# The order of two small GpSimd steps in a software-pipelined attention stage: scales of the branches and scale of the second norm

## The chip, the cores and the metric

The kernel runs on one core of one Trainium2 chip. The metric is the device time of one execution in microseconds (us), the median of several runs. TensorE is called PE, its weight loads PEld, VectorE DVE, ScalarE ACT, GpSimd POOL, SyncE SP, as in the profile.

## What is computed

The input x is 2 x 2048 x 128 in float32, so 4096 tokens of width 128. The layer is a linear attention block and a mixture of eight experts, each with a modulated norm in front and a gate behind:

```python
h = _layernorm(x) * (1 + ca) + sa
# attention block
q = h @ Wq;  feat = elu(q) + 1
msg = (feat @ KV) * Z            # KV and Z from sums over all tokens of a batch
msg = msg @ Wm
y   = h + _layernorm(msg, g1, b1)
mlp = relu(msg @ W1) @ W2
y   = y + _layernorm(mlp, g2, b2)
x   = x + ga * y
# expert block
h = _layernorm(x) * (1 + cb) + sb
x = x + gb * experts(h)          # 8 experts, one per token, chosen from softmax(h @ Wg)
```

The two layernorms inside the attention block (of `msg` and of `mlp`) are the two branches. The kernel needs, for each token, one scale 1/sqrt(mean square + eps) per branch, and then, from the finished x, the mean and the scale of the second norm.

## The kernel before, in words

The 4096 tokens are 32 tiles of 128 (one token per partition), in G = 8 groups of GT = 4 tiles. A first loop over the groups does the first norm, q and the features, and sums what KV needs. The **second loop**, which the change touches, is written out per engine as a software pipeline: each engine has a Python loop over rounds s, and in round s each step of that engine works on a group that is some rounds behind. The engines meet only at semaphores, and each engine runs its own list strictly in the order written. Behind the loop come the router (logits, softmax, a search of ten steps on DVE and ACT for the experts' thresholds), the placing of tokens in slots, and the expert stage with 28 gathers, 35 weight pieces and 28 scatters. None of these is edited.

The steps of the second loop, by group g:

- `qprime(g)` (POOL, L344 to L351) scales the features by z and gives `qp`; PE transposes it (`p_tq`), ACT copies it (`a_qT`, L492).
- PE: `p_y1(g)` (L749) makes branch 1 in bank pQ0, and behind it the hidden layer (L755); `p_y2(g)` (L766) makes branch 2. `p_y1(g)` waits for `u1_done` of group g-1.
- ACT: `a_square(g, 0)` and `a_square(g, 1)` (L501 to L508, four squares each, whose accumulators fill `ssq`) signal `sq1` and `sq2`; `a_relu(g)` (L498, L499) lies between them. `a_xn3(g)` (L523, four tiles) applies the second norm, and waits for `nm_done`.
- POOL: `yrs(g)` (L353 to L358) makes the branches' scales `yr` from `ssq` once `sq1` and `sq2` of group g are there: a small operation at L274 (`yv`) and a power at L275 (`yr`), 128 x 8. `rs3(g)` (L360 to L362) makes the second norm's scale `rs` from the variance in `mv` once `stats3` of group g is there: L274 (`ve`) and L275 (`rs`), 128 x 4.
- DVE: `v_xn3(g)` (L1115) waits for `rs3` and makes `nm`, minus mean times scale; `v_x1(g)` (L1117 to L1127) waits for `yr_done`, adds the two scaled branches to x (L1122, two passes of four tiles), and then takes the statistics of x (`bn` L977, `mv` L980, signal `stats3`); `v_u1`, `v_u2` (L1105, L1110) scale the branches by the rows of weights and free their PSUM banks.

The order in a round s is, per engine: ACT second norm of s-5, squares of branch 1 of s-2, relu of s-2, squares of branch 2 of s-3. DVE:

```python
if 0 <= s - 5 < G - 2:
    v_xn3(s - 5)
if 0 <= s - 4 < G - 1:
    v_x1(s - 4)
```

then `v_u1(s - 2)` and `v_u2(s - 3)`. So on DVE `nm` of a group stands in front of `x1` of the next group. On POOL a round is `qprime(s)`, `rs3(s - 4)`, `yrs(s - 3)`; in rounds 9 and 10 `yrs` stands in front of `rs3`.

Of the kernel before, what the change touches and what calls it, by code (L numbers as in the profile page):

```python
# [20 lines left out]
G = NT // GT  # L21
# [24 lines left out]
def build(nc, x, Wq, Wm, W1, W2, g1, b1, g2, b2, Wg, EW1, EW2, c, wmod, table, out):  # L46
    with ExitStack() as ctx:
# [8 lines left out]
        def sem(name):  # L56
            return ctx.enter_context(nc.semaphore(name))
# [125 lines left out]
        S = {n: sem(n) for n in names}  # L183
# [7 lines left out]
        def experts_of(engine, i):  # L191
            _, values = nc.values_load_multi_w_load_instructions(eid[0:1, i:min(i + RQ, NI)], engines=[engine])
            return [nc.s_assert_within(v, max(0, k - NP + 1), min(k, E - 1),
                                       skip_runtime_bounds_check_because="a piece's expert is counted from the experts' ends on the chip and"
                                                                         " lies between these for any input")
                    for k, v in enumerate(values, i)]
# [62 lines left out]
        def _(gp):  # L259
# [13 lines left out]
            def rsqrt(dst, src, tmp, scale, eps, width):  # L273
                link(gp.tensor_scalar(tmp, src, scale, eps, ALU.mult, ALU.add))  # L274
                return gp.tensor_tensor(dst, tmp, neghalf[:, 0:width], ALU.pow)  # L275
# [68 lines left out]
            def qprime(g):  # L344
                gp.wait_ge(S["z_done"], g + 1)
                if g >= 2:
                    gp.wait_ge(S["tq"], g - 1)
                gp.wait_ge(S["ft_done"], g + 1)
                gp.tensor_tensor(qp[:, g % 2, :].rearrange("p (t c) -> p t c", c=HD),  # L349
                                 bgroup(feat, g).rearrange("p t (h c) -> p (t h) c", c=HD),  # L350
                                 z[:, g % 2, :].unsqueeze(2).to_broadcast([P, GT * H, HD]), ALU.mult).then_inc(S["qp_done"], 1)  # L351

            def yrs(g):  # L353
                gp.wait_ge(S["sq1"], g + 1)
                gp.wait_ge(S["sq2"], g + 1)
                if g >= RY:
                    gp.wait_ge(S["x1_done"], g - RY + 1)
                rsqrt(yr[:, g % RY, :], ssq[:, g % RY, :], yv[:, g % RY, :], 1.0 / D, LN_EPS, 2 * GT).then_inc(S["yr_done"], 1)  # L358

            def rs3(g):  # L360
                gp.wait_ge(S["stats3"], g + 1)
                rsqrt(rs[:, g, :], mv[:, g, :, 1], ve[:, g, :], 1.0, LN_EPS, GT).then_inc(S["rs3"], 1)  # L362

            def rs3_half(h):
                g, ts = G - 1, slice(2 * h, 2 * h + 2)
                gp.wait_ge(S["stats3"], G + h)
                rsqrt(rs[:, g, ts], mv[:, g, ts, 1], ve[:, g, ts], 1.0, LN_EPS, 2).then_inc(S["rs3"], 1)
# [8 lines left out]
            for s in range(G + 6):  # L376
                if s < G:
                    qprime(s)
                if s == G + 2:
                    yrs(G - 1)  # L380
                if s == G + 1:
                    yrs(G - 2)
                if 0 <= s - 4 < G - 1:
                    rs3(s - 4)
                if s - 4 == G - 1:
                    rs3_half(0)
                    rs3_half(1)
                if 0 <= s - 3 < G - 2:
                    yrs(s - 3)
            gp.wait_ge(S["keys"], 1)  # L390
            for g in range(DG):
                h2tok(g)


            gp.wait_ge(S["slots_done"], 1)
            gp.wait_ge(S["tab_done"], 16 * 2 * G)

            def gather(t):
                gp.indirect_dma_start(row[:, t, :], None, table[:, :], bass.IndirectOffsetOnAxis(gidx[:, t:t + 1], 0)).then_inc(gathered[t], 16)  # L399
# [1049 lines left out]
```

## Time and profile before

| | us |
|---|---|
| median of 3 runs | 280.78 |
| lowest, highest | 280.15, 281.31 |
| the profiled execution, its own time | 277.45 |
| span of the profiled execution (first to last instruction) | 275.7 |

The page gives the busy shares PE 68%, DVE 65%, ACT 45%, POOL 47% of the span. The second loop with `yr` and `rs` runs from about 60 to 119 us; the search follows from 129 us, the gathers from 172 us, and the expert pieces to the end. A timeline row reads: start, duration, engine, line, operation, destination<-sources, shapes, count, and in brackets the idle time of the engine in front and who ended it. Several equal instructions in a row are one row (x4); its duration reaches from the first one's start to the last one's end. An ACT square with an accumulator shows as two rows, the second a read of the accumulator.

### The profile page before, as it was taken

The page shows a single profiled execution, that of the slowest core. Times are in us where ns is not written, and L with a number is a line of the kernel's source. Part 1 is how long each engine was busy: PE and PEld are TensorE (multiplying, and loading weights), DVE is VectorE, ACT ScalarE, POOL GpSimd, SP SyncE. Part 2 cuts the span into 40 slices and gives each one's busy share as a digit, 9 for nine tenths or more (in the row PEclk, how much of TensorE's full clock was granted, in tenths as well). Part 3 has the DMA queues.
Part 4 walks back from the last instruction along what each step waited for, and adds up shares of the span by engine and source line. Part 5 has one row for each costly group of instructions (what it writes and reads, how often), then busy time and mean ns, then how long its engine had stood idle before and what let it go on. Part 6 is the DMA issues. An engine that isn't in the chain of part 4 may idle for free.

```text
span 275.7 us, 4416 instructions
## 1 busy us (share of the span) xinstructions
PE 188.1 (68%) x1151; PEld 147.9 (54%) x1151; DVE 177.9 (65%) x660; ACT 124.2 (45%) x392; POOL 129.9 (47%) x207
## 2 busy tenths in 40 slices
PE   0788989796997797676758697751004995966740
PEld 0546759575776577671526275541004984856640
DVE  2779979999977666948898889900001895433340
ACT  2159964465597777435777642311001342232210
POOL 8737303142555445511995000777771037545572
PEclk9999999999799799555575999997555899899895
DMA  5892000001000000000567100434331334443310
GB/s 156 217 322 69 2 1 2 0 0 39 2 0 1 2 0 1 0 2 0 152 179 210 32 4 0 136 116 132 99 110 51 102 88 139 130 117 115 117 39 29
DMA packets 22009, 20.09 MB, mean 73 GB/s; under 512 B 2464, under 2 KB 19360, under 8 KB 21984
## 3 DMA queue, kind: packets, MB, share of 16 engines
q1 hardware_dynamic: 18752, 14.03, 17.2%
q0 software_dynamic: 2240, 5.51, 6.6%
q10 hardware_dynamic: 992, 0.27, 0.8%
q8 instruction: 10, 0.16, 0.3%
q14 instruction: 15, 0.12, 0.1%
HBM read 13.51 MB, written 6.29 MB: 72 GB/s over the span
## 4 chain that ended last, share of the span: by engine, by line
DVE 36%; PE 31%; another core or an unknown queue 11%; POOL 9%; issue 7%; ACT 4%; POOLq 1%; DVEq 0%
PE pQ L938 7%; PE pH L929 6%; DVE scr L1241 6%; DVE x_sb L1122 5%; DVE bn L977 2%; DVE t L1074 2%; POOL out_dram L402 2%; POOL yr L275 2%; PE pQ L648 2%; PE pH L755 2%; POOL rs L275 2%; DVE x_sb L1075 2%; DVE rows L985 2%; PE pQ L842 1%
## 5 line engine op out<-in xcount | busy, mean ns | idle before, releaser
L402 POOL DMA_INDIRECT out_dram<-rows,gidx x28 | 28.4, 1015 | 34.6 <-DVE rows L1389 28.2
L938 PE MATMUL pQ<-ew,u 128*128 (+1 forms) x140 | 25.6, 311 | 27.7 <-DVE dig L1413 21.0
L399 POOL DMA_INDIRECT rows<-table_dram,gidx x28 | 27.7, 988 | 31.5 <-DVE gidx L1333 23.3
L614 ACT ACTIVATE u<-pH 128x256 f32<-128x256 f32 x35 | 13.5, 386 | 58.5 <-remote 27.4
L938 PEld LDWEIGHTS pQ<-ew,u 128*128 128x128 f32 x140 | 21.4, 218 | 30.2 <-issue 28.3
L929 PE MATMUL pH<-x_sb,hid 128*128 (+1 forms) x140 | 25.7, 313 | 9.1 <-issue 7.9
L1381 DVE SCALAR_TENSOR_TENSOR t<-pQ,wslot,scr 128x128 f32<-128x128 f32 x35 | 12.3, 351 | 26.7 <-PE pQ L938 19.4
L929 PEld LDWEIGHTS pH<-x_sb,hid 128*128 128x128 f32 x140 | 21.5, 220 | 10.8 <-issue 10.7
L349 POOL TENSOR_TENSOR scr<-feat,z 128x512 f32<-128x512 f32 x8 | 9.6, 1202 | 23.0 <-DVE z L1101 23.0
L1365 DVE COPY inv<-pL 128x105 f32<-128x105 f32 x1 | 0.3, 269 | 30.4 <-remote 30.4
L755 PE MATMUL pH<-qT,mall 128*128 128x512 f32 x32 | 17.8, 686 | 0.0
L506 ACT ACTIVATE sqj<-pQ 128x128 bf16<-128x128 f32 x60 | 15.7, 275 | 4.7 <-PE pQ L749 2.4
L274 POOL TENSOR_SCALAR ve<-mv 128x4 f32<-128x4 f32 (+1 forms) x17 | 3.6, 209 | 30.1 <-DVE mv L980 27.7
L275 POOL TENSOR_TENSOR rs<-ve,neghalf 128x4 f32<-128x4 f32 (+1 forms) x17 | 16.6, 977 | 1.4
L523 ACT ACTIVATE rows<-x_sb,nm,rs 128x128 f32<-128x128 f32 x30 | 12.5, 486 | 10.7 <-DVE nm L1115 10.2
L977 DVE BATCH_NORM_STATS2 bn<-x_sb 128x6 f32<-128x128 f32 x60 | 13.1, 281 | 5.3 <-DMA x_sb<-in_L_attn_x_dram 5.1
L766 PEld LDWEIGHTS pQ<-w,hid 128*128 128x128 f32 x112 | 13.8, 193 | 4.0 <-issue 4.0
L1122 DVE SCALAR_TENSOR_TENSOR x_sb<-scr,yr,x_sb 128x128 f32<-128x128 f32 x28 | 11.1, 456 | 7.0 <-POOL yr L275 7.0
L373 POOL TENSOR_TENSOR t<-rows,cbR 128x512 f32<-128x512 f32 x7 | 8.9, 1267 | 11.4 <-DVE khi L1231 10.5
L749 PE MATMUL pQ<-mall,qT 128*128 128x128 f32 x64 | 9.5, 295 | 6.6 <-DVE scr L1105 6.6
L275 POOL TENSOR_TENSOR yr<-yv,neghalf 128x8 f32<-128x8 f32 x8 | 13.5, 1692 | 0.7
L766 PE MATMUL pQ<-w,hid 128*128 128x128 f32 x112 | 13.6, 275 | 0.0
(316 smaller groups left out, 526.9 us busy)
## 6 DMA issues: line engine op xcount, KB each, us to landing
hid<-in_L_ffn_W_dram SPq DMA_DIRECT2D x35, 128.0 KB
table_dram<-x_sb SPq DMA_DIRECT2D x9, 256.0 KB, 2.8
x_sb<-in_L_attn_x_dram SPq DMA_DIRECT2D x8, 256.0 KB, 7.5
table_dram<-rows SPq DMA_DIRECT2D x7, 256.0 KB, 2.3
ew<-in_L_ffn_W_dram SPq DMA_DIRECT2D x2, 512.0 KB, 8.5
w1d<-in_L_ffn_W_dram SPq DMA_DIRECT2D x1, 1024.0 KB, 9.8
rows<-table_dram,gidx POOLq DMA_INDIRECT x28
out_dram<-rows,gidx POOLq DMA_INDIRECT x28
```

What stands on the lines that cost most here:

```text
L275: return gp.tensor_tensor(dst, tmp, neghalf[:, 0:width], ALU.pow)
L399: gp.indirect_dma_start(row[:, t, :], None, table[:, :], bass.IndirectOffsetOnAxis(gidx[:, t:t + 1], 0)).then_inc(gathered[t], 16)
L402: gp.indirect_dma_start(out.rearrange("b l d -> (b l) d"), bass.IndirectOffsetOnAxis(gidx[:, t:t + 1], 0), row[:, t, D:2 * D], None).then_ ...
L506: last = act.activation(sqj[:, g % 2, k * GT + t, :], (y2_bank(g) if k else pQ0)[:, t * D:(t + 1) * D], ACT.Square, accum_out=ssq[:, g % R ...
L614: act.activation(eh[:, i % 2, :], pH[i % 2][:, 0:F], ACT.Gelu).then_inc(S["eh_done"], 1)
L755: mm = te.matmul(pH[f][:, :], mall[:, b, D + f * P:D + (f + 1) * P], qT[:, g % 2, :], start=True, stop=True)
L766: mm = te.matmul(y2_bank(g)[:, t * D:(t + 1) * D], hid[:, g % 2, f, t * P:(t + 1) * P], w2[:, f, :], start=(f == 0), stop=(f == 1))
L929: mm = te.matmul(pH[i % 2][:, f * P:(f + 1) * P], wcur[:, i % RW, f * P:(f + 1) * P], xt[:, bass.ds(i - e, 1), :], start=True, stop=True)
L938: mm = te.matmul(pQ[i % 2][:, 0:D], eh[:, i % 2, f * P:(f + 1) * P], ew[:, bass.ds(e, 1), f * D:(f + 1) * D], start=(f == 0), stop=(f == 1))
L977: last = dve.bn_stats(bn[:, g, t, :], x_sb[:, g * GT + t, :])
L1122: last = dve.scalar_tensor_tensor(x1, u[:, t, :], yr[:, g % RY, n + t:n + t + 1], x1, ALU.mult, ALU.add)
L1241: last = dve.tensor_scalar(junk[:, j, :], keys, cur[:, k, j:j + 1], None, ALU.is_lt, ALU.add, accum_out=cnt[:, j:j + 1])
```

## The change

In every round the branches' scales of group s-3 are made in front of the second norm's scale of group s-4. Rounds 9 and 10 had that order, and round 3 has no `rs3`; so the order changes in rounds 4 to 8. Beside it, two waits in front of the first gather change places with each other.

```diff
             for s in range(G + 6):
                 if s < G:
                     qprime(s)
-                if s == G + 2:
-                    yrs(G - 1)
-                if s == G + 1:
-                    yrs(G - 2)
+                if 0 <= s - 3 < G:
+                    yrs(s - 3)
                 if 0 <= s - 4 < G - 1:
                     rs3(s - 4)
                 if s - 4 == G - 1:
                     rs3_half(0)
                     rs3_half(1)
-                if 0 <= s - 3 < G - 2:
-                    yrs(s - 3)
             gp.wait_ge(S["keys"], 1)
             for g in range(DG):
                 h2tok(g)
 
 
+            gp.wait_ge(S["tab_done"], 16 * 2 * G)
             gp.wait_ge(S["slots_done"], 1)
-            gp.wait_ge(S["tab_done"], 16 * 2 * G)
```

POOL's list, rounds 5 and 6 in front of `qprime` of round 6 (L349 writes `qp`, which lies in `scr`; `pool` is the wait of the power for the operation in front of it). Before:

```order
L349 TENSOR_TENSOR scr<-feat,z 128x512 [waits ft_done,tq,z_done]
L274 TENSOR_SCALAR ve<-mv 128x4 [waits stats3]
L275 TENSOR_TENSOR rs<-ve,neghalf 128x4 [waits pool]
L274 TENSOR_SCALAR yv<-ssq 128x8 [waits sq2,sq1]
L275 TENSOR_TENSOR yr<-yv,neghalf 128x8 [waits pool]
```

The same place now:

```order
L349 TENSOR_TENSOR scr<-feat,z 128x512 [waits ft_done,tq,z_done]
L274 TENSOR_SCALAR yv<-ssq 128x8 [waits sq2,sq1]
L275 TENSOR_TENSOR yr<-yv,neghalf 128x8 [waits pool]
L274 TENSOR_SCALAR ve<-mv 128x4 [waits stats3]
L275 TENSOR_TENSOR rs<-ve,neghalf 128x4 [waits pool]
```

In each of the rounds 4 to 7 the pair of `yr` has moved in front of the pair of `rs`. POOL's list from `rs` of round 8 to `rs` of round 10 (there is no `qprime` any more), before:

```order
L274 TENSOR_SCALAR ve<-mv 128x4 [waits stats3]
L275 TENSOR_TENSOR rs<-ve,neghalf 128x4 [waits pool]
L274 TENSOR_SCALAR yv<-ssq 128x8 [waits x1_done,sq2,sq1]
L275 TENSOR_TENSOR yr<-yv,neghalf 128x8 [waits pool]
L274 TENSOR_SCALAR yv<-ssq 128x8 [waits x1_done,sq2,sq1]
L275 TENSOR_TENSOR yr<-yv,neghalf 128x8 [waits pool]
L274 TENSOR_SCALAR ve<-mv 128x4 [waits stats3]
L275 TENSOR_TENSOR rs<-ve,neghalf 128x4 [waits pool]
```

and now:

```order
L274 TENSOR_SCALAR yv<-ssq 128x8 [waits x1_done,sq2,sq1]
L275 TENSOR_TENSOR yr<-yv,neghalf 128x8 [waits pool]
L274 TENSOR_SCALAR ve<-mv 128x4 [waits stats3]
L275 TENSOR_TENSOR rs<-ve,neghalf 128x4 [waits pool]
L274 TENSOR_SCALAR yv<-ssq 128x8 [waits x1_done,sq2,sq1]
L275 TENSOR_TENSOR yr<-yv,neghalf 128x8 [waits pool]
L274 TENSOR_SCALAR ve<-mv 128x4 [waits stats3]
L275 TENSOR_TENSOR rs<-ve,neghalf 128x4 [waits pool]
```

Here only round 8's two pairs have changed places; the pairs of round 9 stand as before. The lists of PE, ACT, DVE and SP are the same in both kernels.

## Rows read from the trace of the kernel before

**Rows 1.** The page's head and its chain that ended last, by engine.
```profile
span 275.7 us, 4416 instructions
...
DVE 36%; PE 31%; another core or an unknown queue 11%; POOL 9%; issue 7%; ACT 4%; POOLq 1%; DVEq 0%
```

**Rows 2.** The page's costliest groups: busy, mean ns | idle before, and its releaser.
```profile
L523 ACT ACTIVATE rows<-x_sb,nm,rs 128x128 f32<-128x128 f32 x30 | 12.5, 486 | 10.7 <-DVE nm L1115 10.2
...
L1122 DVE SCALAR_TENSOR_TENSOR x_sb<-scr,yr,x_sb 128x128 f32<-128x128 f32 x28 | 11.1, 456 | 7.0 <-POOL yr L275 7.0
```

**Rows 3.** Timeline of POOL, round 5: start, us, operation, [idle before <-releaser].
```profile
76.64 0.20 POOL L274 TENSOR_SCALAR ve<-mv 128x4 f32<-128x4 f32 x1 [3.52 <-DVE mv L980]
...
78.02 0.20 POOL L274 TENSOR_SCALAR yv<-ssq 128x8 f32<-128x8 f32 x1
78.30 1.64 POOL L275 TENSOR_TENSOR yr<-yv,neghalf 128x8 f32<-128x8 f32 x1
79.90 1.06 POOL L349 TENSOR_TENSOR scr<-feat,z 128x512 f32<-128x512 f32 x1
```

**Rows 4.** Timeline of DVE, 71 to 110 us.
```profile
71.86 0.10 DVE L1115 SCALAR_TENSOR_TENSOR nm<-mv,rs 128x4 f32<-128x4 f32 x1
...
76.17 0.38 DVE L980 BATCH_NORM_AGGREGATE mv<-bn 128x2 f32<-128x6 f32 x4
...
78.13 0.10 DVE L1115 SCALAR_TENSOR_TENSOR nm<-mv,rs 128x4 f32<-128x4 f32 x1
79.97 1.92 DVE L1122 SCALAR_TENSOR_TENSOR x_sb<-scr,yr,x_sb 128x128 f32<-128x128 f32 x4 [1.74 <-POOL yr L275]
...
84.01 0.38 DVE L980 BATCH_NORM_AGGREGATE mv<-bn 128x2 f32<-128x6 f32 x4
...
95.68 1.14 DVE L1122 SCALAR_TENSOR_TENSOR x_sb<-scr,yr,x_sb 128x128 f32<-128x128 f32 x4 [1.84 <-POOL yr L275]
...
101.12 0.16 DVE L1115 SCALAR_TENSOR_TENSOR nm<-mv,rs 128x4 f32<-128x4 f32 x1
...
109.63 0.16 DVE L1115 SCALAR_TENSOR_TENSOR nm<-mv,rs 128x4 f32<-128x4 f32 x1 [2.09 <-POOL rs L275]
```

**Rows 5.** Timeline of ACT, 72 to 106 us.
```profile
72.00 1.66 ACT L523 ACTIVATE rows<-x_sb,nm,rs 128x128 f32<-128x128 f32 x4 [4.77 <-DVE nm L1115]
...
76.43 0.25 ACT L506 ACTIVATION_READ_ACCUMULATOR sqj<-pQ 128x1 f32 x1
...
78.27 1.66 ACT L523 ACTIVATE rows<-x_sb,nm,rs 128x128 f32<-128x128 f32 x4
...
82.87 0.22 ACT L506 ACTIVATION_READ_ACCUMULATOR sqj<-pQ 128x1 f32 x1
...
101.31 1.65 ACT L523 ACTIVATE rows<-x_sb,nm,rs 128x128 f32<-128x128 f32 x4
...
105.94 0.22 ACT L506 ACTIVATION_READ_ACCUMULATOR sqj<-pQ 128x1 f32 x1
```

**Rows 6.** Timeline of POOL, round 9.
```profile
106.31 0.20 POOL L274 TENSOR_SCALAR yv<-ssq 128x8 f32<-128x8 f32 x1 [3.61 <-issue]
...
108.31 0.20 POOL L274 TENSOR_SCALAR ve<-mv 128x4 f32<-128x4 f32 x1
```

**Rows 7.** Timeline of PE, rounds 7 and 8.
```profile
85.11 1.13 PE L749 MATMUL pQ<-mall,qT 128*128 128x128 f32 x8 [1.48 <-DVE scr L1105]
86.08 1.88 PE L755 MATMUL pH<-qT,mall 128*128 128x512 f32 x4
...
92.99 1.60 PE L749 MATMUL pQ<-mall,qT 128*128 128x128 f32 x8 [1.52 <-DVE scr L1105]
94.37 3.14 PE L755 MATMUL pH<-qT,mall 128*128 128x512 f32 x4
```

**Rows 8.** Windows: length, busy (instructions) of PE, PEld, DVE, ACT, POOL, then PE clock.
```profile
94.00:96.00 2.00, 2.00 (x5) 1.05 (x5) 0.32 (x2) 2.00 (x9) 1.64 (x1) 0.50 0.03 8
```

**Rows 9.** Timeline of POOL, the first gather.
```profile
171.99 1.24 POOL L399 DMA_INDIRECT rows<-table_dram,gidx  x1 [23.27 <-DVE gidx L1333]
```

## The prediction

> **What bounds the kernel now.** I read the page's chain first: DVE carries most of it, and no engine is busy throughout [rows 1], so this is a kernel of waits and every stage is read by itself. Then the costliest groups: DVE's two passes that finish x waited 7.0 us for `yr`, and ACT's second norm waited some 10 us for `nm` [rows 2]. Both are in the second loop, and both waits end at POOL. The timelines of round 5 show how. POOL gets the statistics of group 1 and makes `rs(1)` from 76.64 on, then `yr(2)` from 78.02 to 79.94 [rows 3], and DVE starts `x1(2)` at 79.97 after 1.74 us of waiting [rows 4]. So the loop before is x1, statistics, rs, yr, x1. The reader is to see one more thing: `nm(1)` went out at 78.13, while POOL was still making `yr(2)` [rows 4], and ACT began its second norm at 78.27 [rows 5]. `rs` first gives ACT a start of almost 2 us on DVE.
>
> **What the change costs, step by step.** It adds and removes no operation. It moves five pairs: yr(1) to yr(5) now stand in front of rs(0) to rs(4). POOL waits in order, so `rs` is now held by all that `yr` waits for, that is by ACT's squares of both branches. DVE's list is unchanged and has `nm(g-1)` in front of `x1(g)`; so `x1(g)` still can't start before `rs(g-1)` is made. From one group to the next DVE needs both pairs either way. Their sum stays 3.32 us: from `yv` at 106.31 to `rs`'s first operation at 108.31 is 2.00 [rows 6], and from there to `nm` at 109.63 is 1.32 [rows 4, 6]. What changes is what the pairs wait for, and when ACT may go on.
>
> *Durations.* From `nm` to ACT's second norm 0.15 (78.13 to 78.27 [rows 4, 5]). From the second norm to the end of the squares of branch 2, with relu and the squares of branch 1 between, 4.68 (72.00 to 76.43 + 0.25 [rows 5]). Rounds 6 and 9 took 4.82 and 4.85 (78.27 to 83.09, 101.31 to 106.16 [rows 5]); I take 4.68, since in the other two ACT was early and had PE's branch 2 to wait for, and keep 4.85 as the upper bound. From the last square to `yv` 0.15 (106.16 to 106.31 [rows 5, 6]). Then 3.32.
>
> *Round 4.* yr(1) goes early, under DVE's own work. rs(0) may end some tenths later; `nm(0)` at 71.86 stands behind other DVE work by then. Cost 0.
>
> *Round 5.* ACT starts its second norm at 72.00 as before and ends the squares at 76.68, 0.13 behind the end of the statistics (76.17 + 0.38 = 76.55 [rows 4, 5]). So yr(2) starts at 76.83, and `nm(1)` goes out at 80.15 in place of 78.13: x1(2) is late by 0.3, but the second norm of ACT by 2.0.
>
> *Rounds 6 to 9.* Now a loop closes through ACT: `nm`, second norm, squares, yr, rs, `nm`. Its period is 0.15 + 4.68 + 0.15 + 3.32 = 8.30. In round 6 before, the squares of group 3 were done at 83.09, 1.3 ahead of the statistics at 84.39 [rows 4, 5]. That lead, which would have made the new order pay, was the gift of an early `nm`, and goes with it. DVE doesn't bind: from `nm` to the statistics is 4.5 (79.97 to 84.39, and 0.1), below the 4.83 of ACT. **One row shows the new period already:** in round 9 `yr` stands in front, and from `nm(4)` at 101.12 to `nm(5)` at 109.63 are 8.51 us, with 2.09 of DVE waiting for `rs` [rows 4].
>
> *Sum.* From `nm(0)` at 71.86 (unchanged) to `nm(5)` are five periods. Before: 109.63 - 71.86 = 37.77, or 7.55 each [rows 4]. After: 5 x 8.30 = 41.50, `nm(5)` at 113.36. **The loop ends 3.7 us later.** With 8.51 for each it would be 4.8. With POOL's answer to the squares as quick as to the statistics (76.55 to 76.64, 0.09 for my 0.15 [rows 3, 4]) it is 8.24 each and 3.4. I take 3.6, between the last and the first. Behind `nm(5)` the order is as before, and each stage waits for the one in front: POOL's first gather waited 23.27 us for the slots' addresses from DVE [rows 9], so the delay passes on whole. The two waits in front of that gather are both needed, and their order costs nothing; the later one decides.
>
> *A rule against the trace.* `qprime` ran beside the first pass of x1(2), which took 1.92 us; without it, in group 4, the pass took 1.14 [rows 3, 4]. The collision stays in the new order, as `qprime` and x1 are both released by the end of POOL's second pair, and costs the same 0.78 in both kernels. The Trainium skill (SBUF — State Buffer, Who interferes with whom) says that a VectorE operation with two SBUF inputs and a GpSimd operation that reads SBUF exclude each other, and the later one blocks for the whole instruction. With `nm` now between `rs` and x1, `qprime` (1.06 [rows 3]) would surely be first, and by the rule groups 2 and 3 would each lose up to 0.28 more: the sum would be 4.2 in place of 3.6. The trace shows 0.78 and I keep it.
>
> **Forecast.** The profiled execution took 277.45 and would take 281.05. The runs shown have a median 3.33 above it; a shift in one stage adds to either, so the time is 280.78 + 3.6 = **284.4 us**. A measurement of this kernel can tell some 0.5% (1.4 us) from no change.
>
> **Rivals.**
> - *The scales leave DVE's loop, faster.* The place is the wait of x1 for `yr`. If the squares of group g are done over 2.0 us ahead of the statistics of g-1, yr costs nothing, and the loop is x1, statistics, rs: 4.42 + 0.09 + 1.32 + 0.1 = 5.9, or DVE's own work of about 6.2 (from `nm(0)` to `nm(1)` 6.27 with hardly a wait [rows 4]). All the 7.0 us of waiting [rows 2] would go: 273.8. It decides at a lead of zero: above, x1 gains it, below it loses. For it: a lead of 1.3 in round 6. Against: round 5's lead is -0.13, and every later one comes from an earlier `nm`. Chance 0.05.
> - *No change.* The later second norm hides in ACT's waiting (some 10 us [rows 2]), or the delay is lost in the gathers. Then x1's 0.3 of round 5 is all: 281.1. Against: round 9 shows the period with ACT's waiting gone. Chance 0.08.
> - *Slower by more.* PE waits longer between groups and is granted its lower clock once or twice more. In round 8 it had stood for 1.52, and its clock was 0.50 of full speed (1.2 GHz) at 94 to 96 us [rows 7, 8]; the two steps took 1.60 and 3.14 in place of 1.13 and 1.88, 1.73 more [rows 7]. In round 7 it had stood for 1.48 and kept the clock. One more such stretch, mostly hidden as ACT is the later one, costs 0 to 1.7; with the long period of 8.51 that is 4.8 to 6.5: 285.6 to 287.3, and I put 286.0. Chance 0.14.
> - *The forecast*, 284.4 (its own range 283.6 to 285.6: 3.4 to 4.8, less 0.6 at the low end for the spread of the runs). Chance 0.73.
>
> **Range and chances.** The low end is the forecast's with the short period, 284.2, less 2.0, since the runs shown spread over 1.2 and the profiled one lies 3.3 below them; the high end is the middle of the third rival: 282.2 to 286.4. It leaves out the first two rivals and part of the third. Faster by over 0.5%: 0.05. Within: 0.08. Slower by over 0.5%: 0.87.
>
> **What would show it.** In the profile after: yr(2) starts at about 76.8 right behind ACT's squares; rs follows each yr without a gap; DVE's waits at L1122 for `yr` are gone, and in their place stand waits at L1115 for `rs` of about 2 us in rounds 6 to 9; x1 starts 0.1 behind `nm`; the periods of `nm` are 8.2 to 8.5; ACT's wait for `nm` is longer per round, with nothing of PE ending last at its squares; the stage from `nm(5)` to the end is as long as before. Wrong would be: squares done ahead of the statistics by 1 us or more in rounds 6 to 8, or a second loop as long as before.

## The result, and the profile after

| | before | after |
|---|---|---|
| median of 4 runs each, same chip (us) | 281.04 | 287.22 |
| lowest, highest | 280.15, 281.52 | 285.95, 287.81 |
| the profiled execution, its own time | 277.45 | 287.81 |
| its span | 275.7 | 286.1 |

The ratio is 1.0265 [1.0215, 1.0316], with its 95% interval in brackets: slower by 6.2 us, where 3.6 was forecast. In the experiments below, executions over 1.5% longer than the fastest of the same kernel are left out of medians and ratios, and of three kernels whose profiled execution was such a one (`qprime_gate`, `best`, `best_2`) only stages are read from it, not the whole time.

The spans differ by 10.4, but before was profiled in an execution 3.6 below its median and after in one 0.6 above its own; 10.4 - 3.6 - 0.6 is the same 6.2.

The page after; the first line is the chain that ended last, by engine, and answers to [rows 1]; the second is the group of ACT's second norm, which answers to [rows 2]:

```profile
DVE 20%; PE 15%; another core or an unknown queue 13%; issue 5%; ACT 3%; POOL 2%; DVEq 1%; DMA 1%; POOLq 0%; SPq 0%; ACTq 0%
...
L519 ACT ACTIVATE rows<-x_sb,nm,rs 128x128 f32<-128x128 f32 x30 | 12.4, 484 | 19.7 <-DVE nm L1111 19.4
```

The chain sums to some 60% here and to 100% before, so its shares can't be set against each other, and I read stage by stage. The second line can: ACT now waits 19.4 us for `nm` in place of 10.2. DVE's group of the x1 passes, which waited 7.0 us for `yr`, no longer stands among the page's costliest groups. The waiting went from DVE's x1 to ACT's second norm, as foretold.

The timeline of POOL after, rounds 5 and 6, against [rows 3]:

```profile
77.12 0.20 POOL L274 TENSOR_SCALAR yv<-ssq 128x8 f32<-128x8 f32 x1 [3.70 <-ACT sqj L502]
77.40 1.64 POOL L275 TENSOR_TENSOR yr<-yv,neghalf 128x8 f32<-128x8 f32 x1
79.12 0.20 POOL L274 TENSOR_SCALAR ve<-mv 128x4 f32<-128x4 f32 x1
79.41 1.01 POOL L275 TENSOR_TENSOR rs<-ve,neghalf 128x4 f32<-128x4 f32 x1
80.38 1.06 POOL L349 TENSOR_TENSOR scr<-feat,z 128x512 f32<-128x512 f32 x1
86.32 0.20 POOL L274 TENSOR_SCALAR yv<-ssq 128x8 f32<-128x8 f32 x1 [4.88 <-ACT sqj L502]
```

POOL waits for the squares of ACT, `rs` follows `yr` without a gap, and `qprime` (L349) follows `rs` without a gap. The timeline of DVE after, against [rows 4]; the passes of x1 in rounds 7 to 9, all 1.13, are left out:

```profile
72.15 0.10 DVE L1111 SCALAR_TENSOR_TENSOR nm<-mv,rs 128x4 f32<-128x4 f32 x1
...
80.45 1.01 DVE L1111 SCALAR_TENSOR_TENSOR nm<-mv,rs 128x4 f32<-128x4 f32 x1 [2.21 <-POOL rs L275]
81.38 1.13 DVE L1118 SCALAR_TENSOR_TENSOR x_sb<-scr,yr,x_sb 128x128 f32<-128x128 f32 x4
...
89.65 1.01 DVE L1111 SCALAR_TENSOR_TENSOR nm<-mv,rs 128x4 f32<-128x4 f32 x1 [2.28 <-POOL rs L275]
...
98.85 0.16 DVE L1111 SCALAR_TENSOR_TENSOR nm<-mv,rs 128x4 f32<-128x4 f32 x1 [2.75 <-POOL rs L275]
...
107.19 0.16 DVE L1111 SCALAR_TENSOR_TENSOR nm<-mv,rs 128x4 f32<-128x4 f32 x1 [2.75 <-POOL rs L275]
...
115.54 0.16 DVE L1111 SCALAR_TENSOR_TENSOR nm<-mv,rs 128x4 f32<-128x4 f32 x1 [2.75 <-POOL rs L275]
```

Here is the first thing that the prediction had wrong. The periods of `nm` are 8.30, 9.20, 9.20, 8.34 and 8.35. Three are the forecast's 8.30. The other two are 0.9 longer, and each begins with an `nm` that took **1.01** us where it takes 0.10 or 0.16 elsewhere. The two long ones are those with a `qprime` in front: it started at 80.38, `nm` at 80.45, and both end at 81.4. The x1 pass behind it then took 1.13, not the 1.92 of [rows 4]. `qprime` now hits the small operation that stands first, and ACT waits for that one. Timeline of ACT after, against [rows 5]:

```profile
81.50 1.65 ACT L519 ACTIVATE rows<-x_sb,nm,rs 128x128 f32<-128x128 f32 x4 [3.04 <-DVE nm L1111]
```

It starts 1.05 behind the start of `nm`; before, 78.13 to 78.27 was 0.14 [rows 4, 5]. The five periods sum to 43.39 against 37.77: **+5.6** in place of the forecast's +3.6 or +3.7.

The second thing stands at the gathers, against [rows 9]; timelines of DVE and of POOL after:

```profile
178.95 0.21 DVE L1329 TENSOR_REDUCE gidx<-pG 128x28 int32<-128x56 f32 x1
...
220.22 0.27 DVE L1361 COPY inv<-pL 128x105 f32<-128x105 f32 x1 [33.25 <-remote]
```

```profile
180.06 1.47 POOL L395 DMA_INDIRECT rows<-table_dram,gidx  x1 [25.44 <-DVE gidx L1329]
```

and of DVE before, the operation that makes the addresses and the later one at the slots' inverse table `inv`:

```profile
171.47 0.21 DVE L1333 TENSOR_REDUCE gidx<-pG 128x28 int32<-128x56 f32 x1
...
209.89 0.27 DVE L1365 COPY inv<-pL 128x105 f32<-128x105 f32 x1 [30.40 <-remote]
```

The first gather starts 1.11 behind the start of `gidx` after, and 0.52 before (171.47 to 171.99 [rows 9]), and takes 1.47 for 1.24. So the exchanged waits delay the first gather by 0.6, where I had put nothing. 5.6 + 0.6 = 6.2 is the difference of the medians, but that is a fit and not a measurement: the two profiled executions also differ by 1.6 from `nm(5)` to `gidx` (61.84 and 63.41) and by 3.0 from `gidx` to the first scatter (table below), and neither kernel was profiled again on this chip. The 5.6 of the loop is shown; how the rest of the 6.2 splits is not.

### The profile page after: what moved, and what is told of

Read it like the earlier page. It is cut to its first block, busy times and chain, and to the rows that moved or that the text cites. A ratio compares the mean times of both kernels' runs of the same rounds, so it can differ in the third digit from the quotient of the medians.

```text
span 286.1 us, 4416 instructions
## 1 busy us (share of the span) xinstructions
PE 198.0 (69%) x1151; PEld 153.4 (54%) x1151; DVE 178.4 (62%) x660; ACT 123.0 (43%) x392; POOL 129.0 (45%) x207
## 4 chain that ended last, share of the span: by engine, by line
DVE 20%; PE 15%; another core or an unknown queue 13%; issue 5%; ACT 3%; POOL 2%; DVEq 1%; DMA 1%; POOLq 0%; SPq 0%; ACTq 0%
DVE scr L1237 5%; PE pQ L934 4%; PE pH L925 4%; POOL out_dram L398 2%; DVE scr L1355 1%; PE pQ L838 1%; PE pG L762 1%; DVE u L1397 1%; PE pQ L828 1%; DVE x_sb L1130 1%; DVE x_sb L1118 1%; DVE featT L1321 1%; PE pF L828 1%; DVE cur L1251 1%
## 5 line engine op out<-in xcount | busy, mean ns | idle before, releaser
L925 PE MATMUL pH<-x_sb,hid 128*128 (+1 forms) x140 | 26.9, 323 | 22.6 <-issue 19.6
L925 PEld LDWEIGHTS pH<-x_sb,hid 128*128 128x128 f32 x140 | 22.2, 226 | 24.2 <-issue 23.9
L349 POOL TENSOR_TENSOR scr<-feat,z 128x512 f32<-128x512 f32 x8 | 9.7, 1209 | 25.0 <-DVE z L1097 25.0
L519 ACT ACTIVATE rows<-x_sb,nm,rs 128x128 f32<-128x128 f32 x30 | 12.4, 484 | 19.7 <-DVE nm L1111 19.4
L751 PE MATMUL pH<-qT,mall 128*128 128x512 f32 x32 | 18.4, 707 | 0.0
L274 POOL TENSOR_SCALAR yv<-ssq 128x8 f32<-128x8 f32 x8 | 1.6, 198 | 27.7 <-issue 15.6
L745 PEld LDWEIGHTS pQ<-mall,qT 128*128 128x128 f32 x64 | 8.6, 208 | 8.4 <-issue 7.3
## 6 DMA issues: line engine op xcount, KB each, us to landing
w1d<-in_L_ffn_W_dram SPq DMA_DIRECT2D x1, 1024.0 KB, 10.7
```

Source lines behind the costliest of these rows:

```text
L745: mm = te.matmul(pQ0[:, t * D:(t + 1) * D], qT[:, g % 2, t * P:(t + 1) * P], mall[:, b, 0:D], start=True, stop=True)
L751: mm = te.matmul(pH[f][:, :], mall[:, b, D + f * P:D + (f + 1) * P], qT[:, g % 2, :], start=True, stop=True)
L925: mm = te.matmul(pH[i % 2][:, f * P:(f + 1) * P], wcur[:, i % RW, f * P:(f + 1) * P], xt[:, bass.ds(i - e, 1), :], start=True, stop=True)
```

## The experiments

Four sets of kernels ran, on three chips (A, B twice, C), each set with the kernel before beside it. What follows: medians in us, the ratio to the kernel before on the same chip with its 95% interval.

| kernel | chip | before | this | ratio |
|---|---|---|---|---|
| after_again | A | 275.55 | 286.25 | 1.040 [1.036, 1.045] |
| waits_only | A | 275.55 | 280.38 | 1.019 [1.013, 1.024] |
| qprime_gate | A | 275.55 | 283.74 | 1.031 [1.025, 1.036] |
| turned_yr | A | 275.55 | 277.98 | 1.008 [1.005, 1.011] |
| before_again | B | 275.09 | 277.94 | 1.009 [1.003, 1.014] |
| loop_only | B | 275.09 | 282.32 | 1.024 [1.019, 1.029] |
| waits_memset | B | 275.09 | 281.41 | 1.019 [1.013, 1.025] |
| best | B | 275.09 | 270.51 | 0.983 [0.977, 0.990] |
| after_2 | B | 276.34 | 286.67 | 1.031 [1.024, 1.038] |
| waits_only_2 | B | 276.34 | 280.62 | 1.016 [1.010, 1.021] |
| loop_only_2 | B | 276.34 | 282.98 | 1.016 [1.009, 1.023] |
| best_2 | B | 276.34 | 271.02 | 0.975 [0.968, 0.983] |
| extra_tt | C | 279.78 | 287.58 | 1.023 [1.017, 1.029] |
| waits_three | C | 279.78 | 280.30 | 1.000 [0.995, 1.005] |
| old_waits_memset | C | 279.78 | 279.63 | 0.999 [0.994, 1.003] |
| best_rs_first | C | 279.78 | 279.61 | 0.998 [0.994, 1.002] |

The ratio is taken round by round, and so can differ from that of the medians, by 0.8% in `loop_only_2`. Differences in us below are of the medians, good to some 3 us across labels on chip B; where one carries weight, its ratio stands beside it.

### The two edits apart

`after_again` and `after_2` are the changed kernel. `waits_only` (and `waits_only_2`) is the kernel before with the two waits exchanged alone; `loop_only` (and `loop_only_2`) is the changed kernel with the waits in their old order:

```diff
+            gp.wait_ge(S["tab_done"], 16 * 2 * G)
             gp.wait_ge(S["slots_done"], 1)
-            gp.wait_ge(S["tab_done"], 16 * 2 * G)
```

> The changed kernel itself, beside the kernel before on the same chip. The profiled executions differ by 10.4 us of span, of which 5.6 lie between the first nm and nm(5) (43.39 against 37.77 us), none from nm(5) to the transposes of the probabilities (18.3 both), and 4.5 behind them. Theory A (only the second loop differs): 5.5 to 6.2 us slower, about 286.9 against 281.0; the stretch behind the search differs between executions of one kernel as much as between the kernels. Theory B (the stages behind are slower too): 8 us or more slower.

> The kernel before with only the two waits in front of the first gather in the new order. Theory A: no difference, within 0.3% of before (280.2 to 281.9), since both waits must be met and the slots' addresses come last. Theory B (some of the 6 us comes from there): 0.5 us or more slower.

> The changed kernel with the two waits in front of the first gather in the old order, so only the loop is changed. If the parts add: 5.6 us slower than before (five periods of 43.4 us against 37.8), and the stretch from the addresses to the copy is 38.4 us again. If the waits' order costs nothing and waits_only was chance: as slow as the changed kernel, 10 us on this chip.

> The kernel before, profiled again. If the two waits' order matters by itself (waits_only was 4.8 us slower than before in the median, and from the slots' addresses to the copy of the weights on DVE took 41.06 us there against 38.42), this execution shows again 38.4 us and 0.52 us from the addresses to the first gather. If it was chance, the stretch varies here too, up to 41 us.

On chip A the changed kernel was 10.7 us slower, more than the 6.2 on the first chip, and the exchanged waits alone were 4.8 slower. On chip B `loop_only` cost 7.2 (2.4%). So both edits cost, and the exchange can cost far more than the 0.6 read on the first chip. `before_again`, the same kernel text as the one beside it, came out 0.9% above it on chip B, 2.9 us by the medians: differences of that size across labels I don't read. In one set on chip B the sum was then tried:

> waits_only once more, now on one chip with the three below. Reading so far: with slots_done waited for behind tab_done the first gather starts 1.1 us behind the addresses in place of 0.5, on every chip; the rest of the stage was 4 us longer on two chips and equal on a third, where the kernel before takes 281 and not 276. So: if before takes about 276 here, 4 to 5 us slower; if about 281, 0 to 1 us slower.

> Only the loop changed: 5.6 to 6 us slower than before, whichever chip.

> The changed kernel: 5.6 us for the loop and what waits_only_2 shows: 10 us slower than before if that takes 276, 6.2 us if it takes 281; 286 to 288 in both cases.

+4.3 and +6.6 for the two edits, +10.3 for both; by the ratios 1.6% and 1.6%, and 3.1% for both. They add up, within the spread of a label, and the interval of each `loop_only` ratio holds the 5.6 of the loop. From the profiled executions, stages in us between rows (`nm(0)` to `nm(5)`; `gidx` to the first gather, to the copy `inv` on DVE, and to the first scatter; the last to the end):

| | chip | waits | nm to nm | to gather | to inv | to scatter | to end |
|---|---|---|---|---|---|---|---|
| before | first | old | 37.77 | 0.52 | 38.42 | 53.55 | 50.7 |
| after | first | new | 43.39 | 1.11 | 41.27 | 56.58 | 50.6 |
| before_again | B | old | 37.39 | 0.51 | 27.73 | 52.19 | 50.5 |
| loop_only | B | old | 43.40 | 0.51 | 24.89 | 51.92 | 49.3 |
| waits_only_2 | B | new | 37.72 | 1.11 | 41.01 | 56.25 | 50.4 |
| after_2 | B | new | 43.31 | 1.10 | 41.00 | 55.34 | 49.5 |
| old_waits_memset | C | old | 37.62 | 0.55 | 40.59 | 54.92 | 49.7 |
| waits_three | C | new | 37.81 | 1.10 | 41.25 | 56.51 | 50.8 |

The loop's length depends on the order of the pairs alone and the first gather on the order of the waits alone. Timelines of DVE and of POOL of `loop_only`, the changed loop with the old waits:

```profile
178.55 0.21 DVE L1329 TENSOR_REDUCE gidx<-pG 128x28 int32<-128x56 f32 x1
...
203.44 0.27 DVE L1361 COPY inv<-pL 128x105 f32<-128x105 f32 x1 [16.87 <-remote]
```

```profile
179.06 1.24 POOL L395 DMA_INDIRECT rows<-table_dram,gidx  x1 [24.77 <-DVE gidx L1329]
```

and of `waits_only`, the old loop with the new waits:

```profile
171.10 0.21 DVE L1333 TENSOR_REDUCE gidx<-pG 128x28 int32<-128x56 f32 x1
...
212.16 0.27 DVE L1365 COPY inv<-pL 128x105 f32<-128x105 f32 x1 [33.03 <-remote]
```

```profile
172.21 1.46 POOL L399 DMA_INDIRECT rows<-table_dram,gidx  x1 [23.81 <-DVE gidx L1333]
```

The copy `inv` waits 33 us for something that the trace does not name ("remote") with the new waits, and 16.9 with the old ones on chip B. With the new waits the time from `gidx` to it was 40.9 to 41.3 in all nine profiled executions, on every chip; with the old ones it was 23.4 to 27.7 in five on chip B, 38.4 on the first chip, 40.5 to 40.7 in three on chip C. `before_again` and `loop_only` had been expected to repeat the 38.4 and showed 27.7 and 24.9. So the exchange costs 4 to 5 us where the old order has the short form, and hardly anything where it has the long one anyway. It also fits the kernel before itself, 275 to 276 us on B, 280 on C and 281 on the first chip. That is a pattern over eighteen executions, not a cause; on chip A no kernel with the old waits was profiled.

Two more readings narrow it down. What the copy waits for in the code is the last `pL` matmul of PE. Timelines of PE, of before and then of `loop_only`:

```profile
183.83 0.86 PE L947 MATMUL pL<-featT 128*128 128x105 bf16 x14
```

```profile
190.72 0.86 PE L943 MATMUL pL<-featT 128*128 128x105 bf16 x14
```

By these rows PE was done at 184.7 and 191.6, 25 and 12 us ahead of the copy. So what comes late is not a long matmul but what lies between its row and the signal (the ends of matmuls are modelled). And in the long form the copy starts 2.0 to 4.7 us behind the end of the last gather's issue, in the short form 8.6 to 12.9 ahead of it.

### Does qprime block nm?

`qprime_gate` is the changed kernel, and `qprime` of groups 6 and 7 waits until `nm` has been made:

```diff
             def qprime(g):
+                if g >= 6:
+                    gp.wait_ge(S["nm_done"], g - 4)
```

> The changed kernel, with qprime of rounds 6 and 7 waiting for nm of the group that DVE makes in that round, so that it can't stand in front of nm. Theory A (nm was blocked for qprime's whole 1.06 us, in a loop that runs nm, second norm, squares, yr, rs, nm): nm(1) and nm(2) take 0.1 and not 1.01 us, their periods fall from 9.20 to 8.3, x1's first pass goes back to about 1.9 us but costs nothing, and the kernel is 1.85 us faster than the changed one: 4 us (1.4%) slower than before, 285.0. Theory C (PE's low clock sets the long periods): periods stay at 9.2 in the rounds with the low clock, and the time stays at that of the changed kernel.

Its timeline of DVE:

```profile
83.59 0.16 DVE L1113 SCALAR_TENSOR_TENSOR nm<-mv,rs 128x4 f32<-128x4 f32 x1 [2.18 <-POOL rs L275]
83.67 1.93 DVE L1120 SCALAR_TENSOR_TENSOR x_sb<-scr,yr,x_sb 128x128 f32<-128x128 f32 x4
...
91.94 0.16 DVE L1113 SCALAR_TENSOR_TENSOR nm<-mv,rs 128x4 f32<-128x4 f32 x1 [2.17 <-POOL rs L275]
```

`nm` is back at 0.16, the x1 pass at 1.93: the collision has moved off the loop. The periods are 8.28, 8.35, 8.33, 8.33, 8.33, in sum 41.62, against 41.50 in the prediction. It is 2.5 us faster than `after_again` on the same chip, 1.8 of which is the loop; the other 0.7 is within the spread. With qprime out of the way, the prediction's loop is measured nearly to the tenth.

`extra_tt` does the reverse. The changed loop with the old waits gets, in rounds 8 and 9, which have no `qprime`, one operation of its size whose result nobody uses (extra work, with the output unchanged):

```diff
                 if s < G:
                     qprime(s)
+                if s in (8, 9):
+                    gp.tensor_tensor(t2[:, :, :].rearrange("p t (h c) -> p (t h) c", c=HD),
+                                     bgroup(feat, G - 1).rearrange("p t (h c) -> p (t h) c", c=HD),
+                                     z[:, 1, :].unsqueeze(2).to_broadcast([P, GT * H, HD]), ALU.mult)
```

> The kernel with only the loop changed (loop_only), and in rounds 8 and 9, where there is no qprime, a tensor product of qprime's size and operands into a scratch tile, at qprime's place in POOL's order. It adds work that the reference doesn't have and leaves the output as it is. Theory A (a collision in front of nm costs its whole length in the ACT loop): nm(3) and nm(4) take 1.0 us in place of 0.16, their periods 9.2 in place of 8.35, the kernel 1.75 us slower than loop_only: 8 us slower than before, 284. If POOL's work at that place is free because POOL waits anyway: as loop_only, 282.3.

Its timeline of POOL, and then of DVE:

```profile
98.06 1.06 POOL L380 TENSOR_TENSOR t<-feat,z 128x512 f32<-128x512 f32 x1
```

```profile
98.13 1.01 DVE L1115 SCALAR_TENSOR_TENSOR nm<-mv,rs 128x4 f32<-128x4 f32 x1 [2.74 <-POOL rs L275]
107.30 1.01 DVE L1115 SCALAR_TENSOR_TENSOR nm<-mv,rs 128x4 f32<-128x4 f32 x1 [2.75 <-POOL rs L275]
116.47 0.16 DVE L1115 SCALAR_TENSOR_TENSOR nm<-mv,rs 128x4 f32<-128x4 f32 x1 [2.74 <-POOL rs L275]
```

The two `nm` that took 0.16 in rounds 8 and 9 now take 1.01, and the periods behind them are 9.17 each; the loop is 44.99, 1.6 longer than in `loop_only`. Against before on chip C it is 7.8 us slower by the medians, 6.4 by the ratio; its loop is 7.4 longer than the 37.62 of `old_waits_memset` on that chip. The cause of the missing 1.8 is settled from both sides.

The kernel before shows the same thing on x1. [rows 4] have its pass of four operations as one row of 1.92; a timeline of DVE before that ends at 81.0 us has the first of them alone:

```profile
79.97 1.13 DVE L1122 SCALAR_TENSOR_TENSOR x_sb<-scr,yr,x_sb 128x128 f32<-128x128 f32 x1 [1.74 <-POOL yr L275]
```

The other three took 0.34 each. So the whole collision fell on the one operation that stood first.

### Is it PE's clock?

The rival was a PE that waits longer and gets the lower clock. The hidden layer's four matmuls in rounds 7 and 8 (against [rows 7]), timeline of PE after:

```profile
86.69 1.88 PE L751 MATMUL pH<-qT,mall 128*128 128x512 f32 x4
...
96.77 3.62 PE L751 MATMUL pH<-qT,mall 128*128 128x512 f32 x4
```

and of `loop_only`, rounds 7 to 9:

```profile
86.39 3.39 PE L751 MATMUL pH<-qT,mall 128*128 128x512 f32 x4
...
95.59 1.88 PE L751 MATMUL pH<-qT,mall 128*128 128x512 f32 x4
...
104.16 3.35 PE L751 MATMUL pH<-qT,mall 128*128 128x512 f32 x4
```

Windows of after (the granted clock of PE is the third number from the right) show 1.00 in the first of its two and 0.50 in the second:

```profile
86.70:88.50 1.80, 1.80 (x7) 0.84 (x6) 0.64 (x3) 0.61 (x2) 1.72 (x2) 1.00 0.00 0
97.00:99.00 2.00, 2.00 (x3) 0.78 (x3) 0.15 (x2) 0.00 (x0) 1.65 (x3) 0.50 0.03 8
```

and in `loop_only` the clock was 0.50, 1.00, 0.50 (1.2, 2.4 and 1.2 GHz) at 87 to 89, 96 to 97 and 105 to 107 us. So the low clock fell in other rounds of the two, yet the periods of `nm` are equal: 8.30, 9.21, 9.19, 8.35, 8.35. Between 1.88 and 3.6 for these matmuls the loop doesn't change; ACT and POOL are later. The rival falls for the loop.

### What at the gathers costs 0.6?

Three kernels, all with the loop of before: `waits_memset` has the exchanged waits and a small operation of POOL behind them, `old_waits_memset` the old waits and the same operation, `waits_three` waits for the table, for the slots and for the table again.

```diff
+            gp.wait_ge(S["tab_done"], 16 * 2 * G)
             gp.wait_ge(S["slots_done"], 1)
-            gp.wait_ge(S["tab_done"], 16 * 2 * G)
+            gp.memset(jc[:, 0:1], 0.0)
```

```diff
+            gp.wait_ge(S["tab_done"], 16 * 2 * G)
             gp.wait_ge(S["slots_done"], 1)
             gp.wait_ge(S["tab_done"], 16 * 2 * G)
```

> The kernel before with the two waits in the new order and a memset of one column between them and the first gather. Theory D (a wait for the late signal that sits on the gather itself starts it late, as the engine prepares a gather only when its wait is met): the gather starts about 0.5 us behind the addresses and the time is that of before, 275.6 to 280.8. Theory E (the order of the waits doesn't matter, the long stretch is where instructions of DVE, ACT and PE are fetched behind the gathers' packets and that varies with any shift of the code): the time may be either, and the stretch may be 41 us with the gather starting as early as before.

> The kernel before, its two waits in the old order, and a memset of one column between them and the first gather. It delays the gathers by the memset alone. Theory F: no gain from the late signal's place is lost but the gather starts 0.7 us or more behind the addresses; if a start 0.5 us later alone makes the stage 4 us longer (another meeting of the gathers' packets with the fetches of instructions), the first scatter comes at 56 us; if the carried wait does it, at 52.5 to 54.

> The kernel before, which waits for tab_done, then slots_done, then tab_done again (the third wait is met by then). Five executions with the late signal (slots_done) waited for last began to gather 1.11 us behind the addresses and issued the first scatter 56.2 to 56.6 us behind them; four with tab_done last 0.5 us and 51.9 to 53.5. Theory F (the late signal must not be in the last wait, the one that the next instruction carries): as the old order, 0.5 us and 52 to 53.5 us. Theory G (the place of the late signal in the row of waits counts, not what follows): as the new order, 1.1 and 56.3 us.

From `gidx` to the first gather 1.14, 0.55 and 1.10 us. Timelines of DVE and of POOL of `waits_three`:

```profile
171.34 0.21 DVE L1334 TENSOR_REDUCE gidx<-pG 128x28 int32<-128x56 f32 x1
```

```profile
172.44 1.48 POOL L400 DMA_INDIRECT rows<-table_dram,gidx  x1 [23.84 <-DVE gidx L1334]
```

A memset between the waits and the gather changes next to nothing either way (1.14 and 0.55; I had expected 0.7 or more for the second), which speaks against a wait that is carried by the gather's own instruction. A repeated wait behind the late one doesn't bring back the 0.5 either. What all eighteen profiled executions have in common is one thing: 0.51 to 0.55 where the late signal, `slots_done`, is waited for first, and 1.10 to 1.14 where a wait that is already satisfied stands in front of it. Why stays open. On chip C `waits_three` came out 0.5 above before and `old_waits_memset` 0.2 below, both inside their intervals: there the 0.6 can't be told from nothing. On chip B `waits_memset` cost 1.9%, like `waits_only_2` with 1.6%.

Theory E above, that instructions fetched late set the long stretch, finds no support in the traces. They list the transfers of the `instruction` queues: the last of them in front of the copy `inv` ended 3.4 us ahead of it at the least (`after`), 18.8 in before, and 26.5 and 27.9 in `waits_only_2` and `best_rs_first`, which have the long form.

### An order of ACT and DVE in which the new order pays

If the loop goes through ACT's second norm, taking that off it should help. `turned_yr` is the changed kernel with ACT's second norm behind the squares of branch 1 and relu, and DVE's `v_u1` at the front of a round, so that PE is released earlier:

```diff
-                if 0 <= s - 5 < G - 1:
-                    a_xn3(s - 5)
...
                 if 0 <= s - 2 < G:
                     a_square(s - 2, 0, "y1_ready", "sq1")
                     a_relu(s - 2)
+                if 0 <= s - 5 < G - 1:
+                    a_xn3(s - 5)
...
             for s in range(G + 4):
+                if 0 <= s - 2 < G:
+                    v_u1(s - 2)
...
-                if 0 <= s - 2 < G:
-                    v_u1(s - 2)
```

> The changed kernel, with ACT's second norm moved behind squares of branch 1 and relu in its round, and DVE's scaling of branch 1 (u1) moved to the front of its round. Theory A: the squares no longer wait for nm, they are done ahead of the statistics, and the order of the change then pays: periods of nm of 6.3 to 6.6 us, second loop 4.3 us shorter than before, 276.7 us. Theory C: PE becomes the bound or falls to its low clock more often, and the time is between that of before and that of the changed kernel.

The periods fell to 6.3 to 7.2, in sum 33.40; two `nm` still took 1.05 and 1.06. But `nm(0)` came at 74.39 in place of 72.15, as `v_u1` in front delays the work of the early rounds, and the waits were the new ones: 277.98, still 2.4 above before, where 276.7 had been expected. `best` has the same moves with `v_u1` in front from round 5 on alone, the gate of `qprime`, and the old waits; `best_rs_first` has the moves of ACT and DVE on the kernel before, so `rs` first and no gate.

```diff
             for s in range(G + 4):
+                if s >= 5 and s - 2 < G:
+                    v_u1(s - 2)
...
-                if 0 <= s - 2 < G:
+                if 0 <= s - 2 < 3:
                     v_u1(s - 2)
```

> The order of the change in the loop, the old order of the two waits, ACT's second norm behind relu, DVE's scaling of branch 1 (u1) in front of its round from round 5 on, and qprime of rounds 6 and 7 behind nm. If squares no longer wait for nm, periods of nm are 6.3 us, nm(5) comes 6 us earlier than before, and the kernel is 6 us (2.1%) faster than before. If the old bound only gives way to PE or to its low clock: 3 us or less.

> ACT's second norm behind relu and DVE's u1 in front from round 5 on, as in the best version, but POOL in the old order (rs first; no gate on qprime). The old loop x1, statistics, rs, yr is still closed: periods of x1 of 7.8 us where qprime collides and 7.0 where not, nm(5) within 1 us of before, time 0 to 1 us below before. So the order of the change would be worth 5 us here, and cost 5.6 there. If the re-ordering of ACT and DVE is what gains, this is 4 us or more faster than before.

> The best version once more, in an execution that is not disturbed: 5 to 6 us faster than before, whichever chip, with nm(5) at 105.2 us from the span's start when nm(0) is at 72.

Timeline of DVE of `best_2`:

```profile
80.26 0.16 DVE L1113 SCALAR_TENSOR_TENSOR nm<-mv,rs 128x4 f32<-128x4 f32 x1
...
86.63 0.16 DVE L1113 SCALAR_TENSOR_TENSOR nm<-mv,rs 128x4 f32<-128x4 f32 x1
...
93.00 0.16 DVE L1113 SCALAR_TENSOR_TENSOR nm<-mv,rs 128x4 f32<-128x4 f32 x1 [0.60 <-POOL rs L275]
```

and of `best_rs_first`:

```profile
88.13 1.92 DVE L1122 SCALAR_TENSOR_TENSOR x_sb<-scr,yr,x_sb 128x128 f32<-128x128 f32 x4 [1.73 <-POOL yr L275]
...
95.95 1.14 DVE L1122 SCALAR_TENSOR_TENSOR x_sb<-scr,yr,x_sb 128x128 f32<-128x128 f32 x4 [1.84 <-POOL yr L275]
```

With `yr` first the first period is 7.75 and the other four are 6.33 to 6.37, in which DVE has little left to wait for; the sum is 33.15. With `rs` first DVE again waits 1.7 to 1.8 for `yr` in rounds 7 to 9, as in [rows 4], and the sum is 35.59. `best` is 4.6 and 5.3 us faster than before on chip B, in two sets (0.983 and 0.975), and beats both kernels; `best_rs_first` is level with before on chip C. So `yr` first costs 5.6 us of loop in one surrounding, and in the other, with the gate, it gains 2.4, where the expectation had 5. `turned_yr`, with `yr` first and no gate, has 33.40. Both kernels give some of it back later: from the search's start to `gidx` they take 44.9 to 45.0, `old_waits_memset` 42.3 and `before_again` 43.8. They ran on different chips, and `best` has the gate besides, so how its gain splits is not settled.

## Why the prediction was right and wrong

- **What bounds the kernel.** Right. DVE's waits at x1 went, and ACT's wait for `nm` grew from 10.2 to 19.4 us.
- **Round 5.** `yr(2)` was to start at 76.83 and `nm(1)` to go out 2.0 later, at 80.15. With `nm(0)` at 72.15 in place of 71.86 they came at 77.12 and 80.45: the same to the hundredth or two.
- **The period of 8.30.** Right for the mechanism as costed: 8.30, 8.34 and 8.35 in the rounds without a collision, and 41.62 for all five in `qprime_gate`, for 41.50. The row of round 9 before, 8.51, was the worse guide.
- **"A rule against the trace".** This step failed, and it is the larger miss: +1.8 of the loop. I saw that `nm` now stood between `rs` and x1, and that `qprime` would be first, but priced the collision on x1 alone: 0.78 kept, or 0.28 more per group by the rule. It fell on `nm`, which took 1.01 instead of 0.16, and `nm` is in the loop through ACT, which x1 is not. The cost of the old place doesn't count against it, because x1's share lies beside ACT's work once the loop goes through ACT: in `qprime_gate` the pass took 1.93 and the period stayed at 8.35. By 0.9 for each of two groups the sum would have been 3.7 + 1.8 = 5.5, for 5.6 measured. The Trainium skill (SBUF — State Buffer, Who interferes with whom) says that the later of the two is blocked for the whole instruction; the trace agrees, `nm` ends with `qprime`, at 81.46 and 81.44. It agrees before as well. `qprime` ended at 80.96 [rows 3], and the first x1 operation, alone in its row above, took 1.13 from 79.97 and ended just behind it, where one takes 0.34 otherwise. That is 0.79 more, and the 0.78 was the rule itself. I had read it as something milder.
- **"Their order costs nothing"** (the two waits). Failed: on the first chip the first gather started 0.6 later, and on two others the exchange cost up to 4.8 us. "The later one decides" was true of what is waited for and not of when the gather starts.
- **"The delay passes on whole".** Right within what can be read: from `nm(5)` to the search's start are 19.5 us in every kernel, so the loop's +5.6 arrives at the search whole. That +5.6 and +0.6 make up the +6.2 is a fit, as said with the result. From there to `gidx` the profiled executions vary by more than an edit explains: 42.32 and 43.77 for the same kernel, before and `before_again`.
- **The rivals.** The third had a range of 285.6 to 287.3 and would hold the time of 287.22, but by another mechanism: after has one low-clock stretch in these rounds as before had (96.77, and 94.37 in [rows 7]), and `loop_only`, with two, has the same periods. The first, a loop with the scales out of DVE's way, came near only once ACT's second norm was moved: 6.33 to 6.37 a period, where it said 5.9 to 6.2.

## What to carry to other kernels

Where an order changes, look at which operation now stands first behind a releaser that also releases a large one on another engine: a tiny operation in the critical loop can pay the large one's whole length, and the profile books that as its busy time, not as a wait. Before putting the scale that one engine waits for behind the one that another engine waits for, follow both loops through all engines: the order that loses here shortened the loop once ACT's second norm and DVE's `v_u1` had been moved. And exchange waits only on purpose, with the late signal waited for first as the default here.

## What was not expected of the hardware

- A DVE operation of 128 x 4 took 1.01 us beside a POOL operation of 1.06 with two inputs, and 0.10 or 0.16 without it: in all seven profiled executions of the new order without the gate it was so (1.01 to 1.06) wherever POOL's operation came just in front.
- Two POOL waits in front of an indirect DMA, both needed: with the late one first the DMA started 0.51 to 0.55 behind the producer, with the satisfied one first 1.10 to 1.14, and took 1.24 and 1.44 to 1.48.
- In the gathers' stage DVE waited between 15.4 and 33.3 us for a signal whose sender the trace doesn't name, while by its rows PE had long made what the copy reads; short only on one chip and with one order of the waits. It moves the first scatter by up to 4.7 us. Its cause is open, and so is why the chips differ. Leaving out the wait for the table was not tried, since the gathers would then race with the table's stores.
